# Self attention: which engine copies the token-major head outputs out of their bank

## The chip, the core and the metric

The kernel runs on one core of a Trainium2 chip. The core has TensorE (matrix products, PE in the rows), VectorE (DVE), ScalarE (ACT), GpSimd (POOL) and SyncE (SP, which issues the DMAs). Each engine works through its own queue in order, and engines wait for each other through semaphores. The metric is the device time of one execution in microseconds (us), as the median of some runs.

## What is computed

Four layers follow each other on x of shape (4, 512, 256): attention to a context, a layer of routed experts, a second attention to the context, and self attention whose value and output projections are mixtures of five experts. The change is in the last one, per batch:

```
def _L1_ffn_ref(x, Wq, Wk, Ws, Wd, Wv, Wo):        # h = 8 heads of 64, e = 5 experts
    gl_v = (x @ Ws).reshape(b, t, h, e)
    wv = _topk_mask(gl_v, 2) * sigmoid(gl_v)
    v = einsum('bthe,btek->bhtk', wv, einsum('btd,edk->btek', x, Wv))
    probs = softmax(einsum('bhid,bhjd->bhij', q * scale, k), axis=-1)
    attn = einsum('bhij,bhjd->bihd', probs, v)
    mask_o = _topk_mask((x @ Wd).reshape(b, t, h, e), 2)
    return einsum('bthe,bthk,ekd->btd', mask_o, attn, Wo)
```

x goes through a normalization of its rows first, and the result is added to x.

## The kernel before

`self_layer` works in 16 steps, four per batch of 512 tokens, with one pair of heads in each. Step s of the text is step s of the plan (0 to 15). Within a step the four tiles of 128 keys are taken in turn: scores and their exponentials (`S`, ScalarE writes `probs`), and products with V into the bank `outT` (`AV`). ScalarE then copies `outT` to `OT` (`evac`).

What a pair gives has the head dimension on the partitions. One step later TensorE transposes it, 128x128 four times, into a bank of PSUM (`back`), so that tokens lie on the partitions; this bank is copied to `natural` in SBUF. From `natural` ScalarE (token tiles 0 and 2) and VectorE (tiles 1 and 3) make `masked`: each head times its scale for each of the five experts (`mask`). VectorE adds both heads into `mixed` one step later (`mix`, two additions, one in the first step of a batch). At the end of a batch `mixed` is transposed (`mixT`), projected with Wo and added to X (`out`).

`back` is one of the units that share three banks of PSUM (`ring`), in a fixed order. Others are: the projections `K` and `q`, whose high half ScalarE copies (`KH`, `QH`) and whose rest VectorE then subtracts (`KL`, `QL`); `turn`, the transposed rows of the next batch (`XTH`, `XTL`, likewise); the eight maxima of the next step (`max`, called maxima 0 to 7 in the text: one product of 512 columns each, from which VectorE takes the row maximum into `part`); `sum`, the row sums; and `shift`, the negated maxima (`negtop`), which ScalarE copies to `NM`. A unit can be written once the bank three units earlier has been given back (the semaphores `free`).

One function, `self_plan`, writes the order of the whole layer as a list of items. Every engine walks through this list and executes the items that it has a branch for. So the list sets the order on each queue:

```
        if s:
            front[s * parts].insert(0, ("recip", s - 1))
            put(tail, s, 1, ("back", s - 1), ("mask", s - 1, 0))
            put(tail, s, 2, ("mask", s - 1, 1))
...
        if s > 1:
            put(late, s, 1, ("mix", s - 2))
```

In a step TensorE does: maxima 0 and 1, scores of tiles 0 and 1, `K`, maxima 2 and 3, scores of tiles 2 and 3, products with V of tiles 0 and 1, `back`, maxima 4 and 5, `q`, maxima 6 and 7, products of tiles 2 and 3, the row sums, `shift`. For the row sums VectorE first has to add the `probs` of two key tiles (`acc_dve`), and GpSimd those of the other two. `recip` is the reciprocal of the row sums, ahead of the next step's maxima on VectorE. VectorE normalizes the rows of the next batch in the first step of batches 0 to 2; `turn` comes in the second step of batches 0 to 2, the ranking of the next batch's gates in the third of batches 0 to 2, and `mixT` and `out` of the batch before in the third step of batches 1 to 3.

Of the kernel before, what the change touches and what calls it, by code (L numbers as in the profile page):

```python
# [953 lines left out]
def self_layer(nc, name, x_in, x_out, weights, B, NP, KT):  # L954

    fp32, f32r = mybir.dt.float32, mybir.dt.float32r
    ALU, ACT, AX = mybir.AluOpType, mybir.ActivationFunctionType, mybir.AxisListType
# [30 lines left out]
    with ctx:  # L988
# [151 lines left out]
        @block.scalar  # L1140
        def _(act):
            nc.scalar.preload_act_table_set("natural_log_exp_and_others")
            act.wait_ge(const_made, 1)
            nc.scalar.activation(identr[:, :], ident[:, :], ACT.Copy).then_inc(ident_rounded, 1)
            for item in plan:
                kind = item[0]
                if kind in ("turn", "gate", "q", "K", "shift", "back", "mixT"):
                    bank = bank_of(item)
                    act.wait_ge(full, unit[item] + 1)
                    taken = free[unit[item] % BANKS]  # L1150
                if kind == "wsplit":
                    p = item[1]
                    cols = slice(p * P, (p + 1) * P)
                    act.wait_ge(w_loaded, 32)
                    for ch in range(2):
                        last = nc.scalar.activation(WH[:, ch, :, cols], WRAW[:, ch, :, cols], ACT.Copy)
                    last.then_inc(w_high, 1)
                elif kind == "gsplit":
                    act.wait_ge(g_loaded, 16 * (EXPERTS + 2))
                    nc.scalar.activation(GH[:, :, :], GRAW[:, :, :], ACT.Copy).then_inc(w_high, 1)  # L1160
                elif kind == "turn":
                    _, b, of, ch, g = item
                    nc.scalar.activation(XTH[b % 2][:, ch, :], bank[:, :], ACT.Copy).then_inc(high, 1)
                elif kind == "gate":
                    _, b, t = item
                    if b >= 2 and t == 0:

                        act.wait_ge(v_steps, V_STEPS * NP * (b - 1))
                    nc.scalar.activation(gated[b % 2][:, t, :], bank[:, 0:NGATE], ACT.Copy).then_inc(taken, 1)
                elif kind == "sigm":  # L1170
                    b = item[1]
                    for t in range(QT - BANKS, QT):
                        act.wait_ge(*freed(("gate", b, t)))
                    if b:

                        act.wait_ge(gate_steps, GATE_STEPS * b)
                    nc.scalar.activation(sigm[:, :, :], gated[b % 2][:, :, NV:NV + HEADS * EXPERTS], ACT.Exp, scale=-1.0)\
                      .then_inc(gate_exp, 1)
                elif kind == "q":
                    s = item[1]  # L1180
                    nc.scalar.activation(QH[s % 3][:, :], bank[:, :], ACT.Copy).then_inc(high, 1)
                elif kind == "K":
                    s = item[1]
                    nc.scalar.activation(KH[s % 3][:, :], bank[:, :], ACT.Copy).then_inc(high, 1)
                elif kind == "shift":
                    nc.scalar.activation(NM[item[1] % 2][:, :], bank[:, :], ACT.Copy).then_inc(taken, 1)
                elif kind == "S":
                    _, s, t = item
                    g = tile_no(s, t)
                    act.wait_ge(s_full, g + 1)  # L1190
                    if g >= PROBS:

                        act.wait_ge(av_done, g - PROBS + 1)
                        was, at = divmod(g - PROBS, KT)
                        if at in BY_POOL:
                            act.wait_ge(pool_added, was * POOL_ADDS + max(BY_POOL.index(at), 1))
                        else:
                            act.wait_ge(dve_added, was * DVE_ADDS + max(BY_DVE.index(at), 1))
                    nc.scalar.activation(probs[g % PROBS][:, :, :], scores[g % 2][:, :, :], ACT.Exp, scale=SCALE)\  # L1199
                      .then_inc(exp_done, 1)  # L1200
                elif kind == "evac":

                    s = item[1]
                    act.wait_ge(av_done, tile_no(s + 1, 0))
                    if s >= 2:

                        act.wait_ge(full, unit["back", s - 2] + 1)
                    nc.scalar.activation(OT[s % 2][:, :], outT[:, :], ACT.Copy).then_inc(evacuated, 1)
                elif kind == "back":
                    s = item[1]  # L1210
                    nc.scalar.activation(natural[s % 2][:, :, :, :].rearrange("p t h k -> p (t h k)"), bank[:, :], ACT.Copy)\  # L1211
                      .then_inc(taken, 1)
                elif kind == "mask" and item[2] in (0, 2):
                    _, s, t = item
                    if t == 0:
                        act.wait_ge(*freed(("back", s)))
                        act.wait_ge(scales_made, s + 1)
                        if s >= 2:
                            act.wait_ge(mix_steps, mix_before[s - 1])
                    for e in range(EXPERTS):  # L1220
                        for h in range(2):
                            last = nc.scalar.activation(masked[s % 2][:, t, e, h, :], natural[s % 2][:, t, h, :], ACT.Identity,  # L1222
                                                        scale=scaled[s % 2][:, t, h, e:e + 1], bias=0.0)
                    last.then_inc(rows_masked, 1)
                elif kind == "mixT":
                    t = item[2]
                    nc.scalar.activation(mixedT[:, :, t * P:(t + 1) * P], bank[:, 0:3 * P].rearrange("p (c n) -> p c n", c=3),  # L1227
                                         ACT.Copy).then_inc(taken, 1)

        @block.vector  # L1230
        def _(dve):
# [5 lines left out]
            for item in plan:  # L1237
# [126 lines left out]
                elif kind == "recip":  # L1364
# [8 lines left out]
                    if s >= 2:  # L1373
# [3 lines left out]
                    nc.vector.tensor_tensor(scaled[s % 2][:, :, :, :], gates,  # L1377
                                            recip[:, :, :].unsqueeze(3).broadcast_to([P, QT, 2, EXPERTS]), ALU.mult)\
                      .then_inc(scales_made, 1)
                elif kind == "mask" and item[2] in (1, 3):  # L1380

                    _, s, t = item
                    if t == 1:
                        dve.wait_ge(*freed(("back", s)))
                        dve.wait_ge(scales_made, s + 1)
                        if s >= 2:
                            dve.wait_ge(mix_steps, mix_before[s - 1])
                    nc.vector.tensor_tensor(masked[s % 2][:, t, :, :, :],
                                            natural[s % 2][:, t, :, :].unsqueeze(1).broadcast_to([P, EXPERTS, 2, DH]),
                                            scaled[s % 2][:, t, :, :].rearrange("p h e -> p e h").unsqueeze(3)  # L1390
                                            .broadcast_to([P, EXPERTS, 2, DH]), ALU.mult).then_inc(rows_gated, 1)
                elif kind == "mix":

                    s = item[1]
                    b, p = divmod(s, NP)
                    by = mixed[b % 2][:, :, 0:NV].rearrange("p t (e k) -> p t e k", e=EXPERTS)
                    if p == 0 and b >= 2:
                        dve.wait_ge(full, unit["mixT", b - 2, QT - 1] + 1)
                    dve.wait_ge(rows_masked, 2 * (s + 1))
                    dve.wait_ge(rows_gated, 2 * (s + 1))  # L1400
                    if s:
                        dve.wait_ge(mix_steps, mix_before[s])
                    nc.vector.tensor_tensor(by, by if p else masked[s % 2][:, :, :, 1, :], masked[s % 2][:, :, :, 0, :], ALU.add)\  # L1403
                      .then_inc(mix_steps, 1)
                    if p:
                        dve.wait_ge(mix_steps, mix_before[s] + 1)
                        nc.vector.tensor_tensor(by, by, masked[s % 2][:, :, :, 1, :], ALU.add).then_inc(mix_steps, 1)  # L1407
                elif kind == "out":
                    _, b, t = item
                    dve.wait_ge(x_loaded, 16 * (b + 1))  # L1410
                    dve.wait_ge(full, unit[item] + 1)
                    nc.vector.tensor_tensor(X[:, t, :], bank[:, 0:D], X[:, t, :], ALU.add).then_inc(taken, 1)
# [423 lines left out]
```

## Time and profile before

| What | Value |
|---|---|
| Median of 3 runs | 2548.39 us (2547.73 to 2549.93) |
| The profiled execution, its own time | 2544.89 us |
| Its span, first to last instruction | 2542.9 us |
| Mean granted TensorE clock | 0.944 of full speed |
| Busy share of the span: TensorE, VectorE, ScalarE, GpSimd | 92%, 67%, 46%, 37% |
| The span from 2050 to 2543 us, which holds the self-attention layer: busy us of TensorE, VectorE, ScalarE, GpSimd | 409.0, 360.6, 215.0, 53.0 |
| ScalarE's wait for the transposes of `back` in it | 21.4 us, 15 times |

A busy engine is one that executes; where an engine is not busy, the rows say in brackets how long it was idle and which engine's work ended that. An instruction's time in the rows goes from its start to its end; in a queue the next one can start somewhat earlier than the end, so that a row of two has less than twice the time of one. The granted clock is the share of TensorE's full 2.4 GHz.

### The profile page before, as it was taken

The page shows a single profiled execution, that of the slowest core. Times are in us where ns is not written, and L with a number is a line of the kernel's source. Part 1 is how long each engine was busy: PE and PEld are TensorE (multiplying, and loading weights), DVE is VectorE, ACT ScalarE, POOL GpSimd, SP SyncE. Part 2 cuts the span into 40 slices and gives each one's busy share as a digit, 9 for nine tenths or more (in the row PEclk, how much of TensorE's full clock was granted, in tenths as well). Part 3 has the DMA queues.
Part 4 walks back from the last instruction along what each step waited for, and adds up shares of the span by engine and source line. Part 5 has one row for each costly group of instructions (what it writes and reads, how often), then busy time and mean ns, then how long its engine had stood idle before and what let it go on. Part 6 is the DMA issues. An engine that isn't in the chain of part 4 may idle for free. (4 is left out here: it accounts for less than half of the span.)

```text
span 2542.9 us, 35559 instructions
## 1 busy us (share of the span) xinstructions
PE 2332.5 (92%) x13184; PEld 1499.3 (59%) x13184; DVE 1694.5 (67%) x2966; ACT 1180.1 (46%) x1886; POOL 934.1 (37%) x533
## 2 busy tenths in 40 slices
PE   4999999999999679799999999999999758889897
PEld 3556655665656467565556556655655445556565
DVE  4998798799798477645544554455355237878784
ACT  4566457456555210145553554455354413544454
POOL 3522222222122000157665775676567720101010
PEclk9999999999999879799999999999999977888887
DMA  3000000000000111400000000000000020000000
GB/s 112 19 1 26 17 1 13 31 1 1 11 7 1 43 49 33 130 13 1 1 26 17 1 1 26 17 1 1 3 16 1 1 61 9 1 1 26 17 1 25
DMA packets 62630, 48.59 MB, mean 19 GB/s; under 512 B 12226, under 2 KB 61954, under 8 KB 62466
## 3 DMA queue, kind: packets, MB, share of 16 engines
q1 hardware_dynamic: 62468, 46.40, 6.0%
q8 instruction: 105, 1.72, 0.3%
q14 instruction: 57, 0.47, 0.1%
HBM read 38.01 MB, written 8.39 MB: 18 GB/s over the span
## 5 line engine op out<-in xcount | busy, mean ns | idle before, releaser
L441 POOL TENSOR_TENSOR cross_acc_pool<-cross_acc_pool,cross_probs 128x1024 f32<-128x1024 f32 x192 | 457.7, 2384 | 44.3 <-ACT cross_probs L542 23.3
L661 DVE TENSOR_REDUCE cross_part<-cross_ring 128x1 f32<-128x512 f32 x512 | 323.8, 684 | 139.9 <-PE cross_ring L800 139.8
L427 POOL TENSOR_TENSOR latent_KR<-latent_rot 128x256 f32<-128x256 f32 x128 | 172.7, 1349 | 563.1 <-DVE latent_rot L655 563.1
L542 ACT ACTIVATE cross_probs<-cross_scores 128x1024 f32<-128x1024 f32 x256 | 250.0, 1025 | 100.7 <-PE cross_scores L833 97.0
L542 ACT ACTIVATE latent_probs<-latent_scores 128x1024 f32<-128x1024 f32 x256 | 247.1, 1017 | 74.9 <-PE latent_scores L829 74.9
L689 DVE TENSOR_TENSOR latent_acc_dve<-latent_acc_dve,latent_probs 128x1024 f32<-128x1024 f32 x192 | 258.8, 1348 | 10.4 <-DVE latent_acc_dve L689 0.5
L849 PE MATMUL latent_outT<-latent_probs,latent_VN 128*64 128x512 f32 x1024 | 247.9, 605 | 4.0 <-DVE latent_probs L676 3.9
L849 PE MATMUL cross_outT<-cross_probs,cross_VN 128*64 128x512 f32 x1024 | 247.8, 605 | 0.0
L676 DVE TENSOR_SCALAR latent_probs<-latent_probs 128x2048 f32<-128x2048 f32 x128 | 157.8, 1233 | 25.3 <-ACT latent_probs L542 25.3
L1137 POOL TENSOR_TENSOR self_acc_pool<-self_probs 128x1024 f32<-128x1024 f32 x16 | 39.3, 2458 | 349.6 <-ACT self_probs L1199 349.6
L441 POOL TENSOR_TENSOR cross_acc_pool<-cross_probs 128x1024 f32<-128x1024 f32 x32 | 77.0, 2407 | 227.6 <-PE cross_ring L861 200.2
L722 PE MATMUL latent_ring<-latent_WH,latent_CTH 128*128 128x256 f32 x512 | 156.6, 306 | 1.1 <-DVE latent_newt L698 1.1
L800 PE MATMUL cross_ring<-cross_KH,cross_QH 64*128 64x512 f32 x512 | 137.7, 471 | 12.5 <-DVE cross_KL L634 3.4
L722 PE MATMUL latent_ring<-latent_WL,latent_CTH 128*128 128x256 f32 x512 | 145.1, 283 | 0.0
L722 PE MATMUL latent_ring<-latent_WH,latent_CTL 128*128 128x256 f32 x512 | 145.0, 283 | 0.0
L634 DVE SCALAR_TENSOR_TENSOR cross_KL<-cross_ring,cross_bqkv,cross_KH 128x512 fp32r<-128x512 f32 x64 | 48.0, 751 | 139.6 <-ACT cross_KH L512 139.5
L849 PEld LDWEIGHTS latent_outT<-latent_probs,latent_VN 128*64 128x64 f32 x1024 | 62.1, 136 | 124.0 <-issue 114.8
L800 PEld LDWEIGHTS cross_ring<-cross_KH,cross_QH 64*128 64x128 f32 x512 | 62.0, 185 | 114.0 <-issue 66.8
L520 ACT ACTIVATE latent_VN<-latent_ring 128x256 f32<-128x256 f32 x128 | 49.3, 385 | 167.2 <-PE latent_ring L722 167.2
L722 PEld LDWEIGHTS latent_ring<-latent_WH,latent_CTH 128*128 128x128 f32 x512 | 97.9, 191 | 47.4 <-issue 45.4
L849 PEld LDWEIGHTS cross_outT<-cross_probs,cross_VN 128*64 128x64 f32 x1024 | 62.1, 136 | 102.8 <-issue 84.0
L829 PE MATMUL latent_scores<-latent_QH,latent_KH 64*128 64x512 f32 x512 | 114.4, 444 | 0.0
(296 smaller groups left out, 5534.8 us busy)
## 6 DMA issues: line engine op xcount, KB each, us to landing
latent_C<-in_ctx_dram SPq DMA_DIRECT2D x4, 1024.0 KB, 6.5
cross_C<-in_ctx_dram SPq DMA_DIRECT2D x4, 1024.0 KB, 7.0
latent_XN<-in_x_dram SPq DMA_DIRECT2D x4, 512.0 KB, 3.9
latent_WRAW<-in_L_xattn_Wkv_dram SPq DMA_DIRECT2D x16, 128.0 KB, 2.5
latent_X<-in_x_dram SPq DMA_DIRECT2D x4, 512.0 KB, 3.8
x_after<-latent_X SPq DMA_DIRECT2D x4, 512.0 KB, 2.9
experts_raw<-in_L_ffn_expert_w_dram SPq DMA_DIRECT2D x1, 2048.0 KB
experts_XN<-x_after SPq DMA_DIRECT2D x4, 512.0 KB, 4.0
```

The costliest lines, as they stand in the source:

```text
L427: nc.gpsimd.tensor_tensor(KR[:, 2 * t:2 * t + 2, :], rot1s[n % 2][:, :, :], rot2s[n % 2][:, :, :], ALU.add)\
L441: nc.gpsimd.tensor_tensor(acc_pool[:, :, :], first[:, :, :], probs[g % PROBS][:, :, :], ALU.add)\
L520: nc.scalar.activation(VN[s % 2][:, 2 * t:2 * t + 2, :], src[:, :, 128:256], ACT.Copy).then_inc(v_copied, 1)
L542: nc.scalar.activation(probs[g % PROBS][:, :, :], scores[g % 2][:, :, :], ACT.Exp, scale=SCALE)\
L634: nc.vector.scalar_tensor_tensor(out=L[:, cols], in0=bank[:, :], scalar=bqkv[:, bias, p:p + 1], in1=H[:, cols].bitcast(fp32), op0=ALU.add, ...
L661: nc.vector.reduce_max(part[:, qt, h, i:i + 1], bank[:, :], AX.X).then_inc(taken, 1)
L676: nc.vector.tensor_scalar(both, both, exp(CLIP), exp(-CLIP), ALU.min, ALU.max).then_inc(clipped, 2)
L689: nc.vector.tensor_tensor(acc_dve[:, :, :], first[:, :, :], probs[g % PROBS][:, :, :], ALU.add)\
L722: last = nc.tensor.matmul(out, still, moving, start=i == 0, stop=i == len(passes) - 1)
L800: nc.tensor.matmul(bank[:, :], QH[s % QBUF][HEAD[h], qt * P:(qt + 1) * P], KH[s % 2][HEAD[h], i * 512:(i + 1) * 512], start=True, stop=Tru ...
L829: last = nc.tensor.matmul(scores[g % 2][:, h, :], k[s % 2][HEAD[h], ks], q[s % QBUF][HEAD[h], :], start=i == 0, stop=latent and i == 2)
L849: last = nc.tensor.matmul(outT[HEAD[h], :], V[:, t, at + h * DH:at + (h + 1) * DH], probs[g % PROBS][:, h, :], start=t == 0, stop=t == KT - 1)
```

## The change

The copy of the `back` bank to `natural` is taken out of ScalarE's walk and put into VectorE's, as `tensor_copy`. VectorE waits for the transposes (`full`), and from the third copy on for the masks that ScalarE made of the `natural` buffer's former content (`rows_masked`). The list itself stays. ScalarE's first `mask` of a step, which waits for the bank to be given back, now waits for VectorE.

```
-                if kind in ("turn", "gate", "q", "K", "shift", "back", "mixT"):
+                if kind in ("turn", "gate", "q", "K", "shift", "mixT"):
                     bank = bank_of(item)
                     act.wait_ge(full, unit[item] + 1)
                     taken = free[unit[item] % BANKS]
...
-                elif kind == "back":
-                    s = item[1]
-                    nc.scalar.activation(natural[s % 2][:, :, :, :].rearrange("p t h k -> p (t h k)"), bank[:, :], ACT.Copy)\
-                      .then_inc(taken, 1)
...
+                elif kind == "back":
+                    s = item[1]
+                    dve.wait_ge(full, unit[item] + 1)
+                    if s >= 2:
+
+                        dve.wait_ge(rows_masked, 2 * (s - 1))
+                    nc.vector.tensor_copy(natural[s % 2][:, :, :, :].rearrange("p t h k -> p (t h k)"), bank[:, :])\
+                      .then_inc(taken, 1)
```

In the middle of the layer, in step 7, VectorE's queue held this (`part` is written by the maxima, x2 stands for two in a row):

```order
L1284 TENSOR_TENSOR self_KL<-self_ring,self_KH 128x512
L1388 TENSOR_TENSOR self_masked<-self_natural,self_scaled 128x640
L1288 TENSOR_REDUCE self_part<-self_ring 128x1 x2
L1403 TENSOR_TENSOR self_mixed<-self_mixed,self_masked 128x4x320
L1407 TENSOR_TENSOR self_mixed<-self_mixed,self_masked 128x4x320
L1288 TENSOR_REDUCE self_part<-self_ring 128x1 x2
L1362 TENSOR_TENSOR self_acc_dve<-self_probs 128x1024
L1284 TENSOR_TENSOR self_QL<-self_ring,self_QH 128x512
```

With the change the same place of VectorE's queue reads (line numbers shift with the edit):

```order
L1280 TENSOR_TENSOR self_KL<-self_ring,self_KH 128x512
L1392 TENSOR_TENSOR self_masked<-self_natural,self_scaled 128x640
L1284 TENSOR_REDUCE self_part<-self_ring 128x1 x2
L1382 COPY self_natural<-self_ring 128x512
L1407 TENSOR_TENSOR self_mixed<-self_mixed,self_masked 128x4x320
L1411 TENSOR_TENSOR self_mixed<-self_mixed,self_masked 128x4x320
L1284 TENSOR_REDUCE self_part<-self_ring 128x1 x2
L1358 TENSOR_TENSOR self_acc_dve<-self_probs 128x1024
L1280 TENSOR_TENSOR self_QL<-self_ring,self_QH 128x512
```

The copy has come in between maxima 2 and 3 and the two `mixed` additions; all else keeps its place.

At the end of the layer, in step 15 and behind it, VectorE's queue held:

```order
L1388 TENSOR_TENSOR self_masked<-self_natural,self_scaled 128x640
L1403 TENSOR_TENSOR self_mixed<-self_mixed,self_masked 128x4x320
L1407 TENSOR_TENSOR self_mixed<-self_mixed,self_masked 128x4x320
L1362 TENSOR_TENSOR self_acc_dve<-self_probs 128x1024
L1388 TENSOR_TENSOR self_masked<-self_natural,self_scaled 128x640
L1370 RECIPROCAL self_recip<-self_ring 128x8
L1377 TENSOR_TENSOR self_scaled<-self_rank,self_recip 128x40
```

With the change the same place of VectorE's queue reads:

```order
L1392 TENSOR_TENSOR self_masked<-self_natural,self_scaled 128x640
L1382 COPY self_natural<-self_ring 128x512
L1407 TENSOR_TENSOR self_mixed<-self_mixed,self_masked 128x4x320
L1411 TENSOR_TENSOR self_mixed<-self_mixed,self_masked 128x4x320
L1358 TENSOR_TENSOR self_acc_dve<-self_probs 128x1024
L1392 TENSOR_TENSOR self_masked<-self_natural,self_scaled 128x640
L1366 RECIPROCAL self_recip<-self_ring 128x8
L1373 TENSOR_TENSOR self_scaled<-self_rank,self_recip 128x40
L1382 COPY self_natural<-self_ring 128x512
```

Here the copy of step 15 stands ahead of two `mixed` additions and of the `acc_dve` addition, and the last copy follows behind the scales of step 15.

## Rows read from the trace of the kernel before

**Rows 1.** The page: busy us (share of the span) xinstructions of each engine.

```profile
PE 2332.5 (92%) x13184; PEld 1499.3 (59%) x13184; DVE 1694.5 (67%) x2966; ACT 1180.1 (46%) x1886; POOL 934.1 (37%) x533
```

**Rows 2.** Groups by line and shape, 2050 to 2543 us: busy us, mean ns | idle before.

```profile
L1288 DVE TENSOR_REDUCE self_part<-self_ring 128x1 f32<-128x512 f32 x128 | 82.7, 682 | 13.2 <-PE self_ring L1461 12.6
...
L1211 ACT ACTIVATE self_natural<-self_ring 128x512 f32<-128x512 f32 x16 | 9.6, 598 | 21.4 <-PE self_ring L1516 21.4
...
L1293 DVE TENSOR_SCALAR self_negtop<-self_part 128x512 fp32r<-128x512 f32 x16 | 6.8, 427 | 2.2
```

**Rows 3.** Timeline of VectorE in step 7: start us, us, what, xcount [idle before].

```profile
2307.42 1.28 DVE L1288 TENSOR_REDUCE self_part<-self_ring 128x1 f32<-128x512 f32 x2
2308.62 1.48 DVE L1403 TENSOR_TENSOR self_mixed<-self_mixed,self_masked 128x1280 f32<-128x1280 f32 x1
...
2311.55 1.28 DVE L1288 TENSOR_REDUCE self_part<-self_ring 128x1 f32<-128x512 f32 x2
2312.74 1.22 DVE L1362 TENSOR_TENSOR self_acc_dve<-self_probs 128x1024 f32<-128x1024 f32 x1
```

**Rows 4.** Timeline of ScalarE: the copies of steps 2, 7, 8, 12 and 15.

```profile
2170.04 0.60 ACT L1211 ACTIVATE self_natural<-self_ring 128x512 f32<-128x512 f32 x1 [1.42 <-PE self_ring L1516]
...
2310.20 0.60 ACT L1211 ACTIVATE self_natural<-self_ring 128x512 f32<-128x512 f32 x1 [1.43 <-PE self_ring L1516]
...
2331.48 0.60 ACT L1211 ACTIVATE self_natural<-self_ring 128x512 f32<-128x512 f32 x1 [1.43 <-PE self_ring L1516]
...
2444.22 0.60 ACT L1211 ACTIVATE self_natural<-self_ring 128x512 f32<-128x512 f32 x1 [1.43 <-PE self_ring L1516]
...
2512.39 0.60 ACT L1211 ACTIVATE self_natural<-self_ring 128x512 f32<-128x512 f32 x1 [1.43 <-PE self_ring L1516]
```

**Rows 5.** Timeline of TensorE in step 7: maxima 4, 5; 6, 7; products with V.

```profile
2310.09 0.50 PE L1461 MATMUL self_ring<-self_KH,self_QH 64*128 64x512 f32 x2
...
2312.44 0.94 PE L1461 MATMUL self_ring<-self_KH,self_QH 64*128 64x512 f32 x2
2313.31 1.94 PE L1498 MATMUL self_outT<-self_probs,self_VN 128*64 128x512 f32 x8
```

**Rows 6.** Timeline of VectorE in steps 2, 8, 9, 10 (two rows) and 12.

```profile
2165.73 1.29 DVE L1288 TENSOR_REDUCE self_part<-self_ring 128x1 f32<-128x512 f32 x2
...
2330.59 1.27 DVE L1288 TENSOR_REDUCE self_part<-self_ring 128x1 f32<-128x512 f32 x2
...
2359.51 0.69 DVE L1278 TENSOR_TENSOR self_XTL<-self_ring,self_XTH 128x512 fp32r<-128x512 f32 x1 [4.58 <-ACT self_XTH L1163]
...
2393.01 0.69 DVE L1288 TENSOR_REDUCE self_part<-self_ring 128x1 f32<-128x512 f32 x1 [2.14 <-PE self_ring L1461]
...
2396.22 0.69 DVE L1284 TENSOR_TENSOR self_QL<-self_ring,self_QH 128x512 fp32r<-128x512 f32 x1 [1.40 <-ACT self_QH L1181]
...
2441.99 1.28 DVE L1288 TENSOR_REDUCE self_part<-self_ring 128x1 f32<-128x512 f32 x2
```

**Rows 7.** Timeline of TensorE in steps 1, 2, 6, 8, 12 and 15.

```profile
2146.84 3.68 PE L1498 MATMUL self_outT<-self_probs,self_VN 128*64 128x512 f32 x8
...
2185.71 0.79 PE L1461 MATMUL self_ring<-self_KH,self_QH 64*128 64x512 f32 x1 [4.14 <-DVE self_recip L1370]
...
2279.73 0.49 PE L1461 MATMUL self_ring<-self_KH,self_QH 64*128 64x512 f32 x1 [2.41 <-ACT self_mixedT L1227]
...
2335.93 1.09 PE L1461 MATMUL self_ring<-self_KH,self_QH 64*128 64x512 f32 x2 [1.92 <-DVE self_part L1288]
...
2446.85 1.10 PE L1461 MATMUL self_ring<-self_KH,self_QH 64*128 64x512 f32 x2 [0.31 <-DVE self_part L1288]
...
2512.28 1.94 PE L1498 MATMUL self_outT<-self_probs,self_VN 128*64 128x512 f32 x8
```

**Rows 8.** Stretches: us, busy us of PE, PEld, DVE, ACT, POOL, then granted clock.

```profile
2281.00:2282.00 1.00, 1.00 (x4) 0.81 (x3) 1.00 (x1) 0.00 (x0) 0.00 (x0) 0.50 0.00 0
...
2337.00:2338.00 1.00, 1.00 (x7) 0.43 (x8) 1.00 (x2) 0.00 (x0) 0.00 (x0) 1.00 0.00 0
```

## The prediction

> **What bounds the kernel now.** I read the busy times first, then the groups of the last layer, then the timelines of its engines step by step. TensorE is busy 92% of the span, VectorE 67%, ScalarE 46% [rows 1]; so only time that TensorE loses counts, and VectorE is the engine that can make it lose some. The change lies wholly in the self-attention layer, the last 490 us. There the copy out of the bank costs ScalarE 598 ns, 16 times [rows 2].
>
> Step 7 shows how the engines interlock. ScalarE copies at 2310.20 [rows 4], as soon as TensorE has transposed. VectorE does not take part: it has reduced maxima 2 and 3 by 2308.62, and fills the time of TensorE's products with the two `mixed` additions, until maxima 4 and 5 at 2311.55 [rows 3]. TensorE writes maxima 4 and 5 at 2310.09, the query projection behind them, and maxima 6 and 7 at 2312.44 [rows 5]. Maximum 6 needs the bank of maximum 4, which VectorE has given back at 2311.55 + 0.68 = 2312.23. So the additions, 2.93 us of VectorE's time (2308.62 to 2311.55), are hidden, and just fit: 0.2 us later they would show.
>
> **What the change does to this order.** The copy now stands on VectorE behind maxima 2 and 3 and ahead of the additions. It waits for the transposes, and with it wait the two additions, maxima 4 and 5, the `acc_dve` addition, the low half of the queries and all that follows. So two things are paid where nothing hides them: the time that VectorE stands still, and the copy.
>
> The copy itself: no row shows VectorE copying a 128x512 bank. A maximum, which reads the same bank, takes 682 ns; `negtop`, which writes 512 columns from SBUF, takes 427 [rows 2]. Two maxima in a row take 1.28 us [rows 3], so one holds the queue for 1.28 - 0.68 = 0.60 us. By `negtop` it would be about 0.60 - (0.68 - 0.43) = 0.35. I take 0.61, because the source is the bank, and keep 0.35 for the low end. The Trainium skill ("VectorE: DVE Perf Modes", section "Why PSUM operands drop a tier") says that an fp32 operand in PSUM holds VectorE to its single rate, where SBUF would give the double; the two rows stand in that relation. By the rule the copy is the 0.61 one; without it the sum below would be 2.6 us smaller.
>
> **Step by step.** Steps are numbered 0 to 15 (four per batch); the copy in step s is of output s - 1.
> - Steps 3, 7, 11: VectorE is free at 2308.62 in step 7, the copy can start at 2310.20: 1.58 us still, and 0.61 for the copy, 2.19. Maximum 4 is then given back at 2314.42 and maximum 5 at 2315.0 instead of 2312.8. Maximum 7 waits for the latter, and the products with V behind it start at about 2315.5, not 2313.31: 2.2 us each, 6.6 together.
> - Step 2: VectorE is free at 2165.73 + 1.29 = 2167.0 [rows 6] (it has one addition here, and ranks the next batch's gates behind it), the copy starts at 2170.04: 3.0 + 0.61. Nearly all of it stays, since VectorE is the late one: TensorE waits 4.14 us for its `recip` at the end of the step [rows 7]. 3.6 us.
> - Steps 4, 8: a normalization sits ahead of maxima 2 and 3, so that VectorE is free (2330.59 + 1.27 = 2331.86) after the transposes (2331.48): no stillness. TensorE already waits 1.92 us for maximum 4 [rows 7], so the copy shows in full: 0.6 each, 1.2.
> - Steps 12, 13: free at 2441.99 + 1.20 = 2443.19, copy at 2444.22: 1.03 + 0.61 = 1.64. TensorE waits 0.31 us for the maxima already [rows 7], so all of it shows: 3.3 together.
> - Steps 1, 5, 9: VectorE waits 4.58 us for ScalarE's `XTH` in any case [rows 6], and the copy fits in. Only the masks of ScalarE start later, by 0.68 - 0.60 = 0.08, and `XTH` behind them. Steps 6, 10, 14: VectorE comes 3.6 us late as in step 2, but waits 2.14 us for maximum 5 and then 1.40 for the queries [rows 6]; what is left is 0.1. About 0.6 for the six.
> - Step 15: the copy at 2512.39 stands ahead of two `mixed` additions and the `acc_dve` addition, for which the row sums wait. That ends at 2512.39 + 0.61 + 2.93 + 1.22 = 2517.15, where the sums could start at 2512.28 + 1.94 = 2514.22 [rows 7]: 2.9 us.
> - Behind step 15: the last copy goes ahead of a mask and two additions on VectorE; they were 0.29 us early, so some 0.5 of the copy's 0.61 shows, with the later masks.
>
> Sum: 6.6 + 3.6 + 1.2 + 3.3 + 0.6 + 2.9 + 0.5 = 18.7 us. What is removed, 16 x 0.6 us of ScalarE, gives nothing back: the masks wait for the same copy.
>
> One more term is the TensorE clock. After a wait of 2.41 us in step 6 [rows 7] the granted clock is 0.50 (1.2 GHz); after the 1.92 us wait of step 8 it is still 1.00 (2.4 GHz) [rows 8]. The new waits of steps 3, 7, 11, 12 and 13 are about 2 us, between these. Eight products with V take 3.68 us at the low level and 1.94 at the high one [rows 5, 7], 1.7 us more. I reckon with two of the five: 3.4. Total 22.1 us.
>
> The profiled execution took 2544.89 us, of which 2.0 lie outside its span of 2542.9; it is 3.5 us under the median of the runs, 2548.39. The sum makes it 2567.0, and the median **2570.5**.
>
> **Rivals.**
> - *VectorE catches up (not slower).* It has idle stretches in every step; if these swallow the delay before TensorE asks for a bank, nothing shows: 2548, or 2548.4 + 2.9 + 0.5 = 2552 if only step 15 and the end stay. It is decided at maximum 6: the delay would have to be under 0.2 us in step 7. Against it: the next idle time on VectorE lies behind maximum 7. 8%.
> - *Only the copies count.* If VectorE could get along without standing still (the transposes coming earlier, because TensorE reaches them earlier than in these rows), 16 x 0.61 = 9.8 us would be the most: 2558. The Trainium skill ("Perfetto Trace Analysis", section "Optimizing Scalar/DVE Operations") says that where VectorE is saturated, work that both can do may go to ScalarE; this change goes the other way, and the rule, which looks at load, would give at most these 9.8 us. Here the queue order adds to it. 12%.
> - *The clock falls in all five steps.* 18.7 + 8.5 = 27 us, and 0.15 more per copy (a slower one, as an operation with two operands) in ten places: 2577. For it: each wait comes ahead of thin work, the row sums. Against it: steps 4 and 8 already wait 1.9 us without it. 16%.
> - *The forecast*, 2564 to 2575: 64%.
>
> **How the numbers follow.** Low end: copies at 0.35 in ten places (-2.6) and no clock term, 16 us, 2564; the second rival takes it to 2560. High end: the third rival with the 2 us of scatter among the runs, 2580. A change under 0.2% (5.1 us) can't be told from none: the first rival holds "same", 0.06, and what chance there is of "faster", 0.02; all others are slower, 0.92.
>
> **What would show it.** Right: VectorE idle ahead of its copy, released by the transposes, 1.6 us in steps 3, 7, 11, 3.0 in steps 2, 6, 10, about 1.0 in 12 and 13, none in 4 and 8; copies of 0.65 to 0.7 us; TensorE's waits for the maxima about 2 us each in steps 3, 7, 11, 12, 13, where they are 0 to 0.3 now; the row sums of step 15 released by `acc_dve`. Wrong: maximum 6 not waiting in step 7; a copy of 0.45 us; or the layer's clock moving so that its spells at 1.2 GHz get fewer, which would give back up to 1.7 us a time.

## The result and the profile after

The changed kernel takes 2585.35 us (median of 4 runs, 2584.85 to 2587.32), the kernel before 2548.73 us (4 runs, 2547.73 to 2549.93): 36.6 us more. The quotient of these two medians is 1.0144; the ratio that is given below for every run, and that is not this quotient, is 1.0151 here (95% interval 1.0138 to 1.0163). The predicted 2570.5 us, and the range up to 2580, are too low. The profiled execution took 2585.0 us with a span of 2583.2, 40.3 us more than that of before.

On the page of the changed kernel (columns as in [rows 1]) TensorE has gained 28.5 us of busy time, VectorE 11.9, ScalarE has lost 10.6:

```profile
PE 2361.0 (91%) x13184; PEld 1518.3 (59%) x13184; DVE 1706.4 (66%) x2982; ACT 1169.5 (45%) x1870; POOL 933.6 (36%) x533
```

It runs the same 13184 products. So part of the loss is no waiting: the same products take longer. VectorE's gain is the 16 copies, 11.0 us.

The groups by line and shape from 2090 us to the end (columns as in [rows 2]) price the copy. It takes 690 ns beside 682 for a maximum, and VectorE stood idle 30.1 us ahead of the 16 copies (8.5 of it in step 15):

```profile
L1284 DVE TENSOR_REDUCE self_part<-self_ring 128x1 f32<-128x512 f32 x120 | 77.4, 682 | 11.5 <-PE self_ring L1465 11.1
L1382 DVE COPY self_natural<-self_ring 128x512 f32<-128x512 f32 x16 | 11.0, 690 | 30.1 <-PE self_ring L1520 30.1
```

VectorE's timeline in step 7 answers to [rows 3]: VectorE stands idle 1.43 us ahead of the copy, with the two `mixed` additions and maxima 4 and 5 behind it.

```profile
2321.05 1.27 DVE L1284 TENSOR_REDUCE self_part<-self_ring 128x1 f32<-128x512 f32 x2
2323.75 0.69 DVE L1382 COPY self_natural<-self_ring 128x512 f32<-128x512 f32 x1 [1.43 <-PE self_ring L1520]
2324.36 1.48 DVE L1407 TENSOR_TENSOR self_mixed<-self_mixed,self_masked 128x1280 f32<-128x1280 f32 x1
2325.87 1.49 DVE L1411 TENSOR_TENSOR self_mixed<-self_mixed,self_masked 128x1280 f32<-128x1280 f32 x1
2327.28 1.28 DVE L1284 TENSOR_REDUCE self_part<-self_ring 128x1 f32<-128x512 f32 x2
```

TensorE's timeline shows what this costs, in steps 4, 7, 12 and 15 (L1465 maxima 6 and 7, L1502 products with V, L1513 row sums, L1472 `shift`):

```profile
2233.99 1.10 PE L1465 MATMUL self_ring<-self_KH,self_QH 64*128 64x512 f32 x2 [2.35 <-DVE self_part L1284]
2235.02 2.81 PE L1502 MATMUL self_outT<-self_probs,self_VN 128*64 128x512 f32 x8
...
2328.02 1.39 PE L1465 MATMUL self_ring<-self_KH,self_QH 64*128 64x512 f32 x2 [1.86 <-DVE self_part L1284]
2329.34 3.68 PE L1502 MATMUL self_outT<-self_probs,self_VN 128*64 128x512 f32 x8
...
2339.80 1.09 PE L1472 MATMUL self_ring<-self_identr,self_negtop 128*128 128x128 f32 x4
...
2478.97 1.09 PE L1465 MATMUL self_ring<-self_KH,self_QH 64*128 64x512 f32 x2 [1.86 <-DVE self_part L1284]
2480.00 1.94 PE L1502 MATMUL self_outT<-self_probs,self_VN 128*64 128x512 f32 x8
...
2553.25 0.44 PE L1513 MATMUL self_ring<-self_ones,self_acc_dve 128*128 128x1 f32 x2 [3.02 <-issue]
```

The waits are as forecast: 1.86 us in step 7 (none before) and in step 12 (0.31 before, [rows 7]), 2.35 in step 4, 3.02 ahead of the row sums of step 15 (the row names no releaser, but VectorE's `acc_dve` addition ends at 2553.15, 0.1 us before them). But in step 7 the eight products with V now take 3.68 us, not 1.94 [rows 5], and the row sums behind them the time from 2332.95 to `shift` at 2339.80, 6.85 us. The stretches of step 7 (columns as in [rows 8]) say why:

```profile
2327.00:2328.00 1.00, 0.00 (x0) 0.00 (x0) 1.00 (x3) 0.46 (x1) 0.00 (x0) 1.00 0.00 0
2328.00:2329.00 1.00, 0.98 (x2) 0.52 (x2) 1.00 (x2) 0.00 (x0) 0.00 (x0) 0.55 0.00 0
...
2343.00:2345.00 2.00, 2.00 (x13) 1.58 (x10) 1.93 (x3) 1.92 (x5) 0.00 (x0) 0.50 0.00 0
...
2345.00:2347.00 2.00, 2.00 (x12) 1.08 (x8) 1.38 (x2) 1.03 (x1) 0.41 (x1) 0.96 0.00 0
```

The granted clock falls from 1.00 to 0.50 (1.2 GHz) as TensorE resumes after the wait, stays there through the row sums, and is back at about 2345 us, in the next step. (A stretch at the low clock is called a spell from here on.) The kernel before has a spell here too, but it begins only near the end of the row sums, at about 2318 us, with no wait of TensorE in the 6 us ahead of it:

```profile
2315.00:2317.00 2.00, 2.00 (x19) 1.82 (x17) 1.86 (x5) 0.60 (x1) 0.00 (x0) 1.00 0.00 0
2317.00:2319.00 2.00, 2.00 (x17) 2.00 (x16) 1.93 (x4) 0.00 (x0) 0.00 (x0) 0.79 0.00 0
```

So step 7 has a spell in both kernels; with the change it begins some 10 us earlier, counted from `shift`. From 2090 us to the end the mean granted clock is 0.82 before and 0.78 after.

All steps, in numbers of the two profiled executions. The length of a step is taken from `shift` to `shift`; AV is the time of the eight products with V behind maxima 6 and 7, "sums" the time from the first row sum to `shift`; "predicted" is the sum of the prediction without its clock term.

| Step | longer by | predicted | wait at maximum 6 after (before) | AV before, after | sums before, after |
|---|---|---|---|---|---|
| 2 | 7.63 | 3.6 | 3.15 (0) | 1.94, 3.68 | 4.98, 6.85 |
| 3 | 0.22 | 2.2 | 1.88 (0) | 1.94, 2.65 | 3.86, 6.85 |
| 4 | 4.59 | 0.6 | 2.35 (1.87) | 1.94, 2.81 | 3.60, 6.85 |
| 7 | 6.74 | 2.2 | 1.86 (0) | 1.94, 3.68 | 4.18, 6.85 |
| 8 | 4.24 | 0.6 | 2.35 (1.92) | 1.94, 2.78 | 3.95, 6.85 |
| 11 | 6.75 | 2.2 | 1.88 (0) | 1.94, 3.68 | 4.27, 6.85 |
| 12 | 1.93 | 1.6 | 1.86 (0.31) | 1.94, 1.94 | 3.59, 3.91 |
| 13 | 2.48 | 1.6 | 1.86 (0.32) | 1.94, 1.94 | 3.59, 3.59 |
| 1, 5, 9 | 0.62, -1.95, -1.05 | 0.3 together | | | |
| 6, 10, 14 | 0.13, 0.12, 2.04 | 0.3 together | | | |
| 15 and the end | 3.35 | 3.4 | | | |

These are 37.8 us; the other 2.5 of the 40.3 stand ahead of the first copy, where the two kernels do the same. In steps 2, 4, 7, 8 and 11 the excess over the sum without the clock term (4.0, 4.0, 4.5, 3.6 and 4.6 us) is close to what AV and sums grew by (3.6, 4.1, 4.4, 3.7, 4.3). In steps 12 and 13, with the same wait and no spell behind it, the forecast fits within 0.9.

### The profile page after: what moved, and what is told of

The parts are those of the page before. It is cut to its first block and busy times, and to the rows that moved or that the text cites. A ratio compares the mean times of both kernels' runs of the same rounds, so it can differ in the third digit from the quotient of the medians.

```text
span 2583.2 us, 35573 instructions
## 1 busy us (share of the span) xinstructions
PE 2361.0 (91%) x13184; PEld 1518.3 (59%) x13184; DVE 1706.4 (66%) x2982; ACT 1169.5 (45%) x1870; POOL 933.6 (36%) x533
```

## The experiments

Theory of the place: VectorE stands at the head of its queue with late work behind it, and TensorE pays for that and for the clock. Its rival, the theory of the load: VectorE just has 11 us more to do. Each run is compared with runs of the kernel before on its own chip (medians 2546.37 to 2546.85 us); differences in us are differences of medians unless said otherwise.

**The wait without the copy.** The kernel before, with VectorE waiting where the changed kernel copies:

```
+                elif kind == "back":
+                    dve.wait_ge(full, unit[item] + 1)
```

> ScalarE copies as before; VectorE only waits for the transposes at the place where the changed kernel has its copy. Place theory (VectorE stands still at the head of its queue, and TensorE then waits at maximum 6): the stillness alone is left, without the 0.61 us of the copy: 3.0 us in step 2, 1.6 in steps 3, 7 and 11, 1.0 in steps 12 and 13, 2.3 in step 15, nothing in 4 and 8, 12 us together: 2561, and up to 2572 if the clock falls in some of these steps as it does in the changed kernel. Load theory (the 16 copies are more work on the fuller of the two engines, and that is the loss): no work is added, 2549.

Measured: 2568.44 us, 1.0084 (1.0066 to 1.0102). More than half of the loss comes without any added work. VectorE's timeline in step 7, where ScalarE copies, shows it idle ahead of the addition:

```profile
2319.67 1.49 DVE L1405 TENSOR_TENSOR self_mixed<-self_mixed,self_masked 128x1280 f32<-128x1280 f32 x1 [1.49 <-PE self_ring L1518]
```

TensorE's, of the same step, shows a shorter wait than the changed kernel's, and again slow products with V behind it. Here the spell is short, and the row sums take 4.01 us:

```profile
2323.34 1.18 PE L1463 MATMUL self_ring<-self_KH,self_QH 64*128 64x512 f32 x2 [1.35 <-DVE self_part L1288]
2324.45 3.49 PE L1500 MATMUL self_outT<-self_probs,self_VN 128*64 128x512 f32 x8
```

In the same execution steps 3, 12 and 13 wait 1.36 us and step 8 waits 1.93 us, and the products behind take 1.94.

**The work without the wait.** The kernel before, in which VectorE reduces maximum 3 twice, 15 times in all, each as long as a copy (0.68 us) and waiting for nothing:

```
+                    if s and (qt, h) == (1, 1):
+                        nc.vector.reduce_max(spare[:, :], bank[:, :], AX.X)
```

> The kernel before, with one more row maximum on VectorE per step (of the bank of maximum 3 into a tile that nobody reads, 0.6 us of the queue), ahead of the mixed additions and without a wait for the transposes. Place theory: it shows only where VectorE is late already: 0.6 in steps 2, 4, 8, 12, 13 and 0.4 in steps 3, 7, 11, about 4 us: 2553, up to 2561 if the clock falls in steps 4 and 8. Load theory: about the whole loss of the changed kernel, over 2570.

Measured: 2555.80 us, 1.0030 (1.0019 to 1.0041). TensorE's timeline in step 7: a wait of 0.38 us and no spell behind it.

```profile
2319.47 1.09 PE L1464 MATMUL self_ring<-self_KH,self_QH 64*128 64x512 f32 x2 [0.38 <-DVE self_part L1291]
2320.49 1.94 PE L1501 MATMUL self_outT<-self_probs,self_VN 128*64 128x512 f32 x8
```

The same VectorE time costs 9 us (5 to 10 by the interval) without the standstill and 37 with it. Not all of the 9 is plain work: in the profiled execution, at 2558.4 one of the slower of the ten, steps 4 and 8, where TensorE waits 1.9 us in the kernel before as well, had a spell.

**The clock held up.** The changed kernel, with 8 to 13 products that nobody reads in place of TensorE's idle time ahead of maximum 6, in steps 2, 3, 4, 7, 8 and 11:

```
+                if kind == "max" and item[2:] == (QT - 1, 0) and FILL.get(item[1] - 1):
...
+                    for _ in range(FILL[was]):
+                        nc.tensor.matmul(scores[tile_no(was, 2) % 2][:, 0, :], QH[was % 3][HEAD[0], 0:P], KH[was % 3][HEAD[0], :],
+                                         start=True, stop=True)
```

> The changed kernel; in steps 2, 3, 4, 7, 8 and 11 TensorE executes 8 to 13 products of 512 columns between the query projection and maximum 6, where it would only wait; they go to a bank of the scores that nobody reads before it is written anew. Clock theory (the wait at maximum 6 makes the clock fall, and the products with V and the row sums behind it run at 1.2 GHz): the row sums of these steps take about 3.6 us again and not 6.85, the products with V 1.94: about 20 us less in the five steps, of which some 3 were given back in the next step, so 2568 (2563 to 2573). If the spells come from something else, for instance from the row sums themselves: 2585 or a little more.

Measured: 2569.31 us, 1.0088 (1.0069 to 1.0107). TensorE's timeline in step 7 shows the eight products, maxima 6 and 7, and the products with V back at 1.94 us:

```profile
2322.93 2.10 PE L1439 MATMUL self_scores<-self_KH,self_QH 64*128 64x512 f32 x8
2324.88 1.09 PE L1472 MATMUL self_ring<-self_KH,self_QH 64*128 64x512 f32 x2
2325.90 1.94 PE L1509 MATMUL self_outT<-self_probs,self_VN 128*64 128x512 f32 x8
```

The products with V take 1.94 us in all six steps, and the mean granted clock from 2090 us on is 0.83. Useless work made the kernel 16 us faster by the ratios ((1.0151 - 1.0088) x 2546.4; with their intervals 10 to 22), 14 by the differences from the kernel before (36.6 and 22.9). So the low clock costs 14 to 16 us of the 37, and the remaining 23 are the waits and copies, for which the prediction had 18.7. Step by step the two agree less well: steps 4, 7, 8 and 11 are 1.2 us longer than before together, where the sum has 5.6; steps 5, 6, 9 and 10 are 4.9 longer, where it has at most 0.6; step 15 and the end 5.2 for 3.4.

**The additions out of the way.** The changed kernel, with the mask and the two `mixed` additions ahead of `KL` on VectorE, so that no late work stands behind the copy:

```
-            put(late, s, 0, ("mask", s - 2, 3))
+            put(before, s, 0, ("mask", s - 2, 3), ("mix", s - 2))
...
-            put(late, s, 1, ("mix", s - 2))
```

> The changed kernel with the fourth mask and the two mixed additions of step s - 2 moved ahead of the low half of the keys on VectorE, where it waits for ScalarE by 1 to 2 us in any case; the copy stays on VectorE at its place. Place theory: VectorE comes to the copy about when the transposes are done, nothing but the copy lies ahead of maxima 4 and 5, the wait at maximum 6 goes in steps 3, 4, 7, 8, 11, 12 and 13, and the clock with it: 2545 (2538 to 2552), no slower than the kernel before. Load theory: VectorE has the same work as in the changed kernel, so 2575 to 2585.

Measured: 2579.14 us, 1.0126 (1.0108 to 1.0145), a miss by 34 us. The waits at maximum 6 went in steps 3, 4, 7, 8, 11, 12 and 13, but others came. Four rows, each of its engine's timeline in step 7; VectorE first:

```profile
2320.03 3.02 DVE L1390 TENSOR_TENSOR self_masked<-self_natural,self_scaled 128x640 f32<-128x640 f32 x1
2323.15 1.49 DVE L1405 TENSOR_TENSOR self_mixed<-self_mixed,self_masked 128x1280 f32<-128x1280 f32 x1
```

GpSimd:

```profile
2319.89 2.48 POOL L1135 TENSOR_TENSOR self_acc_pool<-self_probs 128x1024 f32<-128x1024 f32 x1 [35.77 <-ACT self_probs L1197]
```

TensorE:

```profile
2326.82 0.66 PE L1518 MATMUL self_ring<-self_ident,self_OT 128*128 128x128 f32 x4 [2.32 <-DVE self_KL L1278]
```

A mask of 0.82 us took 3.02: it began during GpSimd's addition and ended 0.68 us after it (2323.05 against 2322.37). Then `KL` was late, and the transposes waited 2.32 us for its bank. The next runs test whether VectorE's addition really stood still for GpSimd's.

**Without GpSimd's addition.** In both runs GpSimd adds 4 columns instead of 1024. They leave out the rest of the addition (`acc_pool` is filled with ones once), so their row sums are not the reference's:

```
-                    nc.gpsimd.tensor_tensor(acc_pool[:, :, :], first[:, :, :], probs[g % PROBS][:, :, :], ALU.add)\
+                    nc.gpsimd.tensor_tensor(acc_pool[:, :, 0:2], first[:, :, 0:2], probs[g % PROBS][:, :, 0:2], ALU.add)\
```

> The kernel with mask and mixed additions moved ahead of KL, with GpSimd's addition cut to 4 columns in the same way. Theory that VectorE stood still beside GpSimd: mask back from 3.02 to 0.82 us, mixed additions at 1.48 throughout, the transposes no longer wait for KL by more than 0.5 us, and the waits at the maxima stay gone: 2550 to 2562 us. Rival, that 3.8 us of work ahead of KL are too much by themselves, since VectorE stood still only 1.9 us there: the transposes still wait 1 to 2 us in most steps, 2570 to 2580.

> The changed kernel with GpSimd's addition of row sums cut from 1024 to 4 columns (it leaves that work out, so the row sums are not the reference's), a control for the next run. If the addition's 2.4 us lie beside other work and hold up nobody: 2583 to 2586 us. If VectorE's additions from SBUF stand still while GpSimd adds, a little comes back, at the masks of 0.88 and 1.36 us for 0.82: 2578 to 2584.

Measured: 2539.66 us for the early order, 0.9974 (0.9964 to 0.9984), 39 us less than with GpSimd's whole addition and below the range expected; 2573.56 us for the control, 1.0107 (1.0090 to 1.0124), 4 us lower than its range. So the small addition gives 10 to 12 us in the changed kernel, and 39 in the early order. In the control's steps 4 and 8 AV stayed at 1.94 us, which was not expected, although TensorE's wait ahead of it is the changed kernel's; TensorE's timeline of step 4:

```profile
2232.34 1.10 PE L1466 MATMUL self_ring<-self_KH,self_QH 64*128 64x512 f32 x2 [2.36 <-DVE self_part L1285]
2233.37 1.94 PE L1503 MATMUL self_outT<-self_probs,self_VN 128*64 128x512 f32 x8
```

In the early order's listing of `mixed` (the columns: ns least/median/most, first and last start) no addition is stretched any more:

```profile
L1406 DVE TENSOR_TENSOR self_mixed<-self_mixed,self_masked x12: 1492/1493/1493, 2190.0 to 2520.1; 128x1280 f32<-128x1280 f32 x12
```

The same listing of the early order with GpSimd's whole addition:

```profile
L1405 DVE TENSOR_TENSOR self_mixed<-self_mixed,self_masked x12: 1491/3516/3522, 2200.5 to 2558.8; 128x1280 f32<-128x1280 f32 x12
```

**GpSimd's addition later.** It may not start before the transposes are done, so that it falls where VectorE reads banks; once in the changed kernel alone, once with the early order, and once with the early order and ScalarE's copy:

```
-                            pool.wait_ge(full, unit["sum", s - 1] + 1)
+                            pool.wait_ge(full, unit["back", s - 1] + 1)
```

> The changed kernel with only GpSimd's addition held back, a control. The waits ahead of the copies and at maximum 6 stay at 1.4 and 1.9 us in step 7; VectorE's own addition may now stand still beside it: 2575 to 2595 us. If holding back GpSimd is by itself what helps: 2560 or less.

Measured: 2606.10 us, 1.0232 (1.0215 to 1.0249), slower than expected: the collision has moved onto the `mixed` additions of the old order. VectorE's timeline in step 7:

```profile
2330.29 0.69 DVE L1382 COPY self_natural<-self_ring 128x512 f32<-128x512 f32 x1 [1.48 <-PE self_ring L1520]
2330.90 3.23 DVE L1407 TENSOR_TENSOR self_mixed<-self_mixed,self_masked 128x1280 f32<-128x1280 f32 x1
2334.17 1.49 DVE L1411 TENSOR_TENSOR self_mixed<-self_mixed,self_masked 128x1280 f32<-128x1280 f32 x1
```

GpSimd's:

```profile
2330.40 2.38 POOL L1137 TENSOR_TENSOR self_acc_pool<-self_probs 128x1024 f32<-128x1024 f32 x1 [35.29 <-PE self_ring L1520]
```

The copy, which reads a bank, keeps its 0.69 us beside GpSimd; the addition of two SBUF operands ends 1.35 us after GpSimd's (2334.13 against 2332.78), about its own length.

> The changed kernel with mask and mixed additions ahead of KL and GpSimd's whole addition held back until the transposes into the bank are done, so that it runs while VectorE reads banks (copy, maxima 4 and 5) and not while it adds in SBUF. Nothing is left out. If VectorE's standstill beside GpSimd was all that the early place cost: mixed additions at 1.49 us throughout, no long wait at maximum 6, 2538 to 2552 us, at or below the kernel before. Rival: the standstill moves on to VectorE's addition of row sums, ahead of QL and maximum 6: that addition 2 to 3 us instead of 1.22, and 2560 to 2575 us.

Measured: 2547.51 us, 1.0008 (0.9998 to 1.0018): the time of the kernel before, with VectorE copying. VectorE's timeline in step 7:

```profile
2306.33 1.49 DVE L1405 TENSOR_TENSOR self_mixed<-self_mixed,self_masked 128x1280 f32<-128x1280 f32 x1
2307.86 1.49 DVE L1409 TENSOR_TENSOR self_mixed<-self_mixed,self_masked 128x1280 f32<-128x1280 f32 x1
...
2311.93 0.69 DVE L1380 COPY self_natural<-self_ring 128x512 f32<-128x512 f32 x1 [0.78 <-PE self_ring L1518]
2312.54 1.28 DVE L1282 TENSOR_REDUCE self_part<-self_ring 128x1 f32<-128x512 f32 x2
```

TensorE's: maxima 6 and 7 without a wait, products with V at 1.94 us.

```profile
2314.28 0.50 PE L1463 MATMUL self_ring<-self_KH,self_QH 64*128 64x512 f32 x2
2314.71 1.94 PE L1500 MATMUL self_outT<-self_probs,self_VN 128*64 128x512 f32 x8
```

> The same order with ScalarE's copy, as in the kernel before. Theory of the place: once VectorE does not stand ahead of the transposes with late work behind it, the copy costs it little, and this run is within 6 us of the one with VectorE's copy. Theory of the load: it is 10 us or more below it.

Measured: 2540.37 us, 0.9975 (0.9965 to 0.9984). So in this order VectorE's copy costs 7.1 us over ScalarE's: more than the place theory allowed (6), less than the load theory asked (10). The two traces, one execution each, say where, from `shift` to `shift`: steps 7 to 13 differ by 0.5 us together, although VectorE copies in each of them. Step 2 is 7.5 us longer: VectorE stands idle 3.03 us ahead of its copy there, TensorE waits, and a spell follows. Steps 3 to 6 give 4.5 of it back. Step 15 and the end are 2.9 longer, for there the copy pushes the `acc_dve` addition beside GpSimd's (2.94 us for 1.22), and the row sums wait for it. Step 1 is 1.0 longer. TensorE's timeline with VectorE's copy, in steps 2 and 15:

```profile
2177.57 1.39 PE L1463 MATMUL self_ring<-self_KH,self_QH 64*128 64x512 f32 x2 [3.01 <-DVE self_part L1282]
2178.88 3.68 PE L1500 MATMUL self_outT<-self_probs,self_VN 128*64 128x512 f32 x8
...
2513.58 0.35 PE L1511 MATMUL self_ring<-self_ones,self_acc_dve 128*128 128x1 f32 x2 [1.82 <-DVE self_acc_dve L1356]
```

So what the copy still costs in this order is again mostly place and clock, not load.

**The copy behind the additions.** The changed kernel, with the copy moved on VectorE alone (in steps 1, 5, 9 and 13 it keeps its place):

```
+    for s in [s for s in range(1, B * NP) if s % NP]:
+        dve_plan.remove(("back", s))
+        dve_plan.insert(dve_plan.index(("mix", s - 1)) + 1, ("back", s))
```

> The changed kernel, but VectorE executes its copy behind the mixed additions instead of ahead of them (steps 1, 5 and 9 keep the old place, where the copy comes ahead of a subtraction that depends on it). The mixed additions then fill the time in which VectorE stood still for the transposes. Theory of the place: copies wait 1.43 us less in steps 7 and 11, 0.8 to 1.2 less in 3, 12 and 13, 1.5 in 2, 2.9 in 15, about 10 us together; TensorE's wait at maximum 6 in steps 7 and 11 falls from 1.86 to about 0.4, and the spells at the low clock behind it go (4.3 us each): 2560 to 2570 us. If the spells stay although the waits shrink: 2575. Theory of the load (0.69 us of copy, wherever it stands): 2585.

Measured: 2571.45 us, 1.0087 (1.0064 to 1.0111), 1.5 us above the range (its four runs spread from 2562.5 to 2573.4). The same copies at another place cost 12 us less. Idle time on VectorE and the wait at maximum 6 are gone in step 7; but `q` uses the bank that the copy empties, and now waits for it. TensorE's timeline, first of the six products of `q`, then maxima 6 and 7:

```profile
2323.94 0.50 PE L1429 MATMUL self_ring<-self_XTH,self_WH 128*128 128x512 f32 x1 [1.78 <-DVE self_natural L1386]
...
2325.51 0.49 PE L1469 MATMUL self_ring<-self_KH,self_QH 64*128 64x512 f32 x2
```

In steps 3, 4, 8 and 12 `q` waits 2.24, 3.03, 3.02 and 2.24 us, and AV takes 2.5 to 3.2 us there. Step 13, where the copy kept its place, has the changed kernel's wait of 1.86 us, and here a spell behind it:

```profile
2489.44 1.39 PE L1469 MATMUL self_ring<-self_KH,self_QH 64*128 64x512 f32 x2 [1.86 <-DVE self_part L1288]
2490.76 3.22 PE L1506 MATMUL self_outT<-self_probs,self_VN 128*64 128x512 f32 x8
```

**Filling waits that both kernels have.** The products that nobody reads, put into the kernel before and into the early order with the late addition:

```
+    FILL = {("q", s + 2): (s, 13) for s in (1, 5, 9)}
+    FILL["max", 15, QT - 2, 1] = 14, 10
```

> The kernel before, with 13 products of 512 columns that nobody reads ahead of q's products in steps 1, 5 and 9, where TensorE waits 3.24 us, and 10 ahead of maximum 5 in step 14, where it waits 2.40. Clock theory: the stretch from q to the row sums, which ran at 0.50 (q's six products 0.63 us for each where 0.40 is the other level, products with V 3.68, 3.35, 3.16 and 3.16 us instead of 1.94), runs at the full clock: about 4 us less in each of 1, 5 and 9 and 1.2 in 14, 2533 to 2541 us. Rival: behind these stretches VectorE, not TensorE, decides, and the faster products only wait longer: 2546 to 2549.

> The first of these with 13 products that nobody reads ahead of q in steps 1, 5 and 9 and 10 ahead of maximum 5 in step 14. Before, such products freed the spell in step 1 for good, but in 5 and 9 only exchanged TensorE's wait ahead of q for one of 1.9 us behind it. Clock theory: 3 to 10 us below the first. Rival, VectorE's work decides there: no difference.

Measured: 2541.62 us for the first, 0.9981 (0.9972 to 0.9991), 0.6 us above the range: step 1 ran at 1.94 us for AV instead of 3.68, but in steps 5 and 9 VectorE's reduction was next to be waited for, and the clock fell again. And step 4, which is not filled, became 5.3 us longer in the profiled execution (the slowest of the ten): behind a wait of 1.77 us, for 1.87 in the kernel before, it had a spell that the kernel before does not have there (AV 3.68 for 1.94). TensorE's timeline of steps 1 and 5:

```profile
2150.11 1.94 PE L1506 MATMUL self_outT<-self_probs,self_VN 128*64 128x512 f32 x8
...
2255.74 0.66 PE L1446 MATMUL self_ring<-self_ident,self_XN 128*128 128x128 f32 x4 [1.88 <-DVE self_part L1290]
...
2258.62 3.44 PE L1506 MATMUL self_outT<-self_probs,self_VN 128*64 128x512 f32 x8
```

The second: 2539.80 us, 0.9976 (0.9967 to 0.9986), 7.7 below the same without the products. This run and the early order with ScalarE's copy beat the kernel before by 6 us, and the changed one by some 45.

## Why the prediction was wrong

- **Right: the mechanism of the waits.** VectorE stands idle ahead of the copy, 1.43 us in step 7, 3.03 in step 2, 0.95 and 1.16 in steps 12 and 13, not at all in 4 and 8. Off was step 3, 0.80 for 1.58. The copy is 0.69 us for the forecast 0.65 to 0.7: the bank sets its price, not `negtop`'s 427 ns. The Trainium skill ("VectorE: DVE Perf Modes", section "Why PSUM operands drop a tier") had said so, and the trace agrees.
- **Right: the waits of TensorE.** 1.86 to 1.88 us in steps 3, 7, 11, 12 and 13, 2.35 in 4 and 8, 3.02 ahead of the last row sums. The sum of 18.7 us answers to the 23 that stay when the clock is held up, with some 4 missing; that it comes so near is in part luck, since the steps agree less well than the total (see that run).
- **Wrong: the clock term, 3.4 us for 14 to 16.** It failed in three ways. It priced only the eight products with V (1.7 us), while the low clock also held through the row sums, to which the prediction gave nothing (4.18 to 6.85 us in step 7). It expected two spells among steps 3, 7, 11, 12 and 13; they came in the first three, and in step 2 as well. And it took steps 4 and 8 as safe, because 1.92 us of wait had passed there without a spell [rows 8]; with 2.35 us the clock fell in both. Behind the last two stands one premise, that the length of the wait tells whether a spell follows, safe at 1.92 us and not at 2.41. The runs speak against it: spells came behind waits of 1.35 us (the wait without the copy, step 7), 1.77 (the kernel before with filling, step 4) and 1.86 (step 7), and none behind 1.93 (the wait without the copy, step 8) and 2.36 (the control with 4 columns, step 4). Not all of the growth stays: steps 5 and 9 became 1.95 and 1.05 us shorter, and in step 3 the wait of 4.14 us for `recip` [rows 7] is gone, since VectorE caught up while TensorE was slow; with the clock held up it is back (4.15 us).
- **The rivals.** That VectorE catches up fell with the wait of 1.86 us at maximum 6 in step 7. That the copies alone count (9.8 us) fell with the wait without copy, 22 us. The load, for which the prediction drew on the Trainium skill ("Perfetto Trace Analysis", section "Optimizing Scalar/DVE Operations"), has its measure in the work without the wait: 9 us, near the 9.8 that the prediction gave it as the most. The rival of the clock (2577) was right that more spells come, but it priced each the same as the forecast did, at 1.7 us, and it had them in steps 12 and 13 too, where they stayed away.

That VectorE's standstill makes TensorE wait, and the size of the clock term, are shown by runs. What decides whether a wait is followed by a spell is not: steps 12 and 13 kept the clock after 1.86 us in the changed kernel, and step 13 lost it after the same 1.86 us with the copy behind the additions. The length of the wait alone does not tell the two apart, and that cause stays open.

## What to carry to other kernels

Before work is moved to an in-order engine, look at what it will wait for there and what stands behind it: here 16 copies of 0.69 us cost 37 us at the head of the queue, and 15 reductions as long cost 9 us as plain work. A wait of 1.4 to 2.4 us on TensorE can cost more than itself: in a forecast, price the products behind it (here those with V and the row sums) at half the clock as the upper bound, and at the full clock as the lower one; products that nobody reads, put into the wait, show in one run how much of a loss is clock. An addition with two SBUF operands on VectorE needs a place where GpSimd doesn't add.

## What the runs showed of the hardware

- The granted clock fell to 0.50 after a wait of 1.86 us (step 7) and stayed there through 10 us of products with V and row sums on a busy TensorE. It fell after 1.35 us too (the wait without the copy, step 7), there for some 3 us, and it held after 1.93 us (the same run, step 8) and 2.36 us (the control with 4 columns, step 4). In the kernel before it fell in the row sums of step 7, at about 2318 us, after 6 us without a wait.
- VectorE's addition of two SBUF operands stands still beside GpSimd's addition: 0.82 us became 3.02, and 1.49 became 3.23 and 3.52; where both ends are shown above, it ended about its own length after GpSimd's (0.68 and 1.35 us). The read of a bank beside it kept its time (the copy 0.69 us). This is the exclusive port pair of the Trainium skill ("SBUF — State Buffer", section "SBUF: two separate sides"), which the plan of the early order had overlooked; the trace agrees.
